# Attention scores of a gated cross-attention block: a second, turned score pass on TensorE replaced by row-wise exp on ScalarE, 32x32 turns on VectorE and block moves in SBUF

## The chip, the cores and the metric

The kernel runs on one NeuronCore of a Trainium2 chip. The metric is the device time of one execution in microseconds (us). The median of three runs of the kernel before is 1319.23 us (1318.6 to 1319.34).

## What is computed

The input x has 8 batches of 512 features by 2048 positions. Cut to what matters:

```python
# xattn: patches of W = 128 positions, H = 8 heads of dh = 32, DK = 256
q, k = Wq @ z + bq, Wk @ z + bk          # z = layernorm(x) over positions
val  = Wv @ ctx + bv
scores = einsum('bhdi,bhdj->bhij', qh, kh) / sqrt(dh)
scores = where(mask > 0, scores, -1e9)
attn = softmax(scores, axis=-1)
o = gelu(einsum('bhij,bhdj->bhdi', attn, vh))
x = x + tanh(g_x) * (Wo @ o + bo) * mask
# ffn: router over the positions of each row of layernorm(x), top 8 of 64 experts
logits = rows @ router.T + rb            # contraction over the 2048 positions
x = x + tanh(g_f) * (rows * w_sum + w_dense @ expert_bias)
```

The softmax of a patch and head is over j, along a row of the score matrix. The product with the values contracts over j, so it wants the weights with j on the partitions. The router contracts over positions, so it wants x with positions on the partitions.

## The kernel before

The work is cut into 64 units (`TU`), each of 256 positions (two patches, w = 0 and 1) of one batch. Eight units make a batch. There are five instruction streams, one for each engine and one for SyncE (SP) which issues the DMAs. Each stream is written in order by a loop over ticks: `SLOTS` gives every stage a place in a unit of 16 slots, unit u comes 16 slots after unit u - 1, and a negative or large number means an earlier or later unit's turn. The places set only the order in which an engine takes its work; the times come from semaphores. `ENDS` moves stages of the last units. Seven PSUM banks go round as a ring (`take`), given out ahead by the same places; `PR` is the eighth.

The stages of one unit, with their lines:

- `z_full` (L1115, GpSimd), `z_high` (L624, ScalarE) and `z_low` (L1122, GpSimd) make the normalised input and its two float32r parts. `project` (L316 to L318, TensorE) forms q and then k, 24 matmuls each; `q_full` (L632, ScalarE) and `k_full` (L806, VectorE) add the biases. The context goes through `c_high` (L640), `c_low` (L1128), `v_mm` (L331 to L333) and `v_full` (L646) the same way, twice per unit.
- `scores` (L347, L355, TensorE): mask rows `sel` times `ones3`, then q by k, 16 score tiles of 128x128 in four banks, query i on the partitions. `top` (L814, VectorE) takes the row maxima, `split` (L823 to L829) cuts them into three bf16 parts, `turn_max` (L367, TensorE) turns them, `max_turned` (L652, ScalarE) evicts them.
- `scores_turned` (L385, L392, TensorE) forms the scores again with key j on the partitions, mask and negated maxima added by matmuls. `expo` (L659, ScalarE) is four exps of 128x512 into `P`. `sums` (L403, TensorE) forms the denominators, `weigh` (L417) the product with the values. `invert` (L835, VectorE) is a reciprocal of 128x512, `divide` (L840) multiplies.
- `gelu` (L664) and `o_high` (L673) on ScalarE, `o_low` (L1139, GpSimd), `project_out` (L436 to L438, TensorE, two halves), `weigh_out` (L851, VectorE) and `add_x` (L1134, GpSimd) update x in place. Exp and gelu each load a table (`ACT_TABLE_LOAD`) in every unit.
- `r_full` (L684, ScalarE) centres the updated x, `r_turn` (L451, TensorE) turns it, `r_high` (L693, ScalarE) and `r_low` (L883, VectorE) split it, `r_mm` (L463, L464) adds it to the router's sum. `stats2` (L864) and `input_stats` (L967) are VectorE's statistics.
- Once per batch: the router's end (`c_logits` to `c_scale`, L699 to L940), `scale_x` (L720, ScalarE, four times 128x2048), `mix` (L500, L501, TensorE, 16 banks) and `add_mix` (L957, VectorE, 16), then 16 stores (L574) and, for the batch after next, 16 loads of x (L569), 256 KB each, issued by SP.

SP also issues per unit four small loads of mask rows into `sel` (L562), one of the mask (L553) and two of the context (L547).

Of the kernel before, what the change touches and what calls it, by code (L numbers as in the profile page):

```python
# [7 lines left out]
BF16 = mybir.dt.bfloat16  # L8
# [6 lines left out]
DT = D // 128  # L15
# [12 lines left out]
def bf16_parts(v):  # L28
# [23 lines left out]
    h=35.75, hT=39.75, hT_gap=0.25, ht_hi=42.25, ht_lo=44.5, R=49.75,  # L52

    norm2=25.25, c_base=28.75, L=33.25, LT=36.75, c_top=35.5, c_exp=37.25, c_w=41.25, c_sc=42.75, wT=40.5, wt_hi=41.25, wt_lo=42.5, mix=44.5, m_gap=0.25,
    sx=44.75, sx_gap=1.5, x2=46.5, rl=54.75, rl_gap=1,

    x_1=10.0, x_gap=3.75, bn1=66.75, bn1_gap=1.75, norm1=96.75,
# [13 lines left out]
G_IDENT, G_MXB = 2, 8  # L71


V_SUM, V_PICK, V_ROWS, V_SEL, V_ONES3, V_IDB, V_BQ = 3, 5, 9, 11, 12, 13, 14
V_KEEP, V_SW = 4, 7

TA = 1


def gated_block_kernel(nc, x, ctx, mask, g_x, g_f, wqT, wkT, wvT, woT, bq, bk, bv, bo, wrT, rb, eb, out):  # L80
    with ExitStack() as st:
# [9 lines left out]
        def f32(ap):  # L91
# [4 lines left out]
        NC, NV, NRW, NR, NO = 2, 4, 3, 7, 3  # L96
# [19 lines left out]
        P = sb("P", [128, 4, 2, 2, W])  # L116
        v32 = [sb(f"v32_{i}", [128, E]) for i in range(NV)]
        mx = [sb(f"mx{i}", [128, 4, 4]) for i in range(2)]
        mr = sb("mr", [128, 4, 4])
        mxb = sb("mxb", [128, 4, 8, 4], BF16)  # L120
        mxT = [sb(f"mxT{i}", [128, W], BF16) for i in range(2)]
        sel = [sb(f"sel{i}", [128, 4, W], BF16) for i in range(NRW)]
        pick = sb("pick", [128, 5])
        ones32 = sb("ones32", [128, DH])
# [3 lines left out]
        hc = [sb(f"hc{i}", [128, DT, U]) for i in range(2)]  # L128
# [9 lines left out]
        idb = sb("idb", [128, 128], BF16)  # L138
# [61 lines left out]
        s_pe, mx_v, part_v, mt_pe, mt_a, st_pe, exp_a, den_pe, pv_pe, rc_v, on_v = (sem(n) for n in (  # L200
            "S", "mx", "part", "MT", "mxT", "ST", "exp", "DEN", "PV", "rc", "on"))
        gelu_a, othi_a, otlo_g, wo_pe, xt_v, x1_g = (sem(n) for n in ("gelu", "othi", "otlo", "WO", "xt", "x1"))
        bn2_v, agg2_v, neg2_v, rstd2_g, h_a, ht_pe, hthi_a, htlo_v, r_pe = (sem(n) for n in (
            "bn2", "agg2", "neg2", "rstd2", "h", "hT", "hthi", "htlo", "R"))
# [6 lines left out]
        TICKS = range(-32 * 8, 8 * (128 * (NB + 1) + 96))  # L211
        SPLIT = -48
# [42 lines left out]
        for t in TICKS:  # L255
            for u in due(t, C["S"]):
                for g in range(4):
                    take(("S", 4 * u + g), t, C["top"] - C["S"] + g / 8, mx_v, 4 * u + g + 1)
# [34 lines left out]
        def _(e):  # L293
# [64 lines left out]
            def turn_max(u):  # L358
                _, freed, n = bank_of["MT", u]
                if freed:  # L360
                    e.wait_ge(freed, n)
# [851 lines left out]
```

## Time and profile before

| | |
|---|---|
| median of three runs | 1319.23 us |
| profiled execution, first to last instruction (span) | 1316.7 us |
| PE (TensorE) busy | 1273.2 us, 97% |
| DVE (VectorE) busy | 1004.8 us, 76% |
| ACT (ScalarE) busy | 893.3 us, 68% |
| POOL (GpSimd) busy | 712.7 us, 54% |
| DMA traffic | 116.15 MB, mean 88 GB/s |

The profiled execution is told by its span; no other time of it is given. The median of the runs is 2.5 us above that span. Busy times are of one engine each and overlap. A matmul's duration includes its way through the array, so the price of a group of matmuls is read from the start of one group to the start of the next.

### The profile page before, as it was taken

What the parts mean: (1) busy time and instruction counts of PE and PEld (TensorE: products, weight loads), DVE (VectorE), ACT (ScalarE), POOL (GpSimd) and SP (SyncE); (2) the same over time, 40 slices, a digit from 0 to 9 for tenths busy, and PEclk for the clock granted to TensorE, in tenths of its full rate; (3) what the DMA queues carried; (4) which work ended last, traced back from release to release, by engine and by line L of the source; (5) the groups of instructions that cost most, each with busy time, mean ns of one, the idle gap of its engine ahead of it and who ended that gap; (6) DMA issues with size and microseconds to landing.
All of it is one profiled execution on the core that took longest, in us unless ns stands there. A gap on an engine that the chain in (4) does not pass through costs nothing.

```text
span 1316.7 us, 37880 instructions
## 1 busy us (share of the span) xinstructions
PE 1273.2 (97%) x15313; PEld 1120.4 (85%) x15313; DVE 1004.8 (76%) x1871; ACT 893.3 (68%) x1600; POOL 712.7 (54%) x662
## 2 busy tenths in 40 slices
PE   3999999999999999999999999999999999999997
PEld 3898888889878889798887899878888798888875
DVE  6669768896788966888678776888768797687677
ACT  4676667677686676766667776676676766686755
POOL 2655664556645665456663655636664556654531
PEclk9999999999999999999999999999999999999999
DMA  9331111811136111451115411153111721123103
GB/s 277 110 104 43 34 42 51 262 40 39 43 102 216 36 39 35 149 170 43 34 43 165 154 32 42 34 192 128 43 35 38 242 78 43 34 78 114 34 6 128
DMA packets 120620, 116.15 MB, mean 88 GB/s; under 512 B 11392, under 2 KB 88320, under 8 KB 120320
## 3 DMA queue, kind: packets, MB, share of 16 engines
q1 hardware_dynamic: 119584, 113.74, 27.7%
q8 instruction: 122, 2.00, 0.6%
q14 instruction: 50, 0.41, 0.1%
q10 hardware_dynamic: 864, 0.01, 0.0%
HBM read 80.06 MB, written 33.65 MB: 86 GB/s over the span
## 4 chain that ended last, share of the span: by engine, by line
PE 84%; DVE 7%; ACT 5%; issue 2%; DMA 1%; POOL 0%; SPq 0%; DVEq 0%; ACTq 0%; POOLq 0%
PE ring L316 9%; PE ring L317 8%; PE ring L318 8%; PE ring L436 5%; PE ring L392 4%; PE ring L403 4%; PE ring L438 4%; PE ring L437 4%; PE ring L355 4%; PE ring L331 4%; PE ring L332 4%; PE ring L333 4%; PE ring L417 4%; PE ring L451 4%; PE PR L463 3%; ACT X L720 2%
## 5 line engine op out<-in xcount | busy, mean ns | idle before, releaser
L316 PE MATMUL ring<-z_hi,wqk_hi 128*128 128x256 f32 x1024 | 297.1, 290 | 21.8 <-DVE z_lo L1029 21.8
L1128 POOL TENSOR_TENSOR cx_lo<-cx,cx_hi 128x512 fp32r<-128x512 f32 x128 | 165.9, 1296 | 262.7 <-ACT cx_hi L640 262.7
L317 PE MATMUL ring<-z_hi,wqk_lo 128*128 128x256 f32 x1024 | 290.5, 284 | 0.0
L318 PE MATMUL ring<-z_lo,wqk_hi 128*128 128x256 f32 x1024 | 290.3, 283 | 0.0
L316 PEld LDWEIGHTS ring<-z_hi,wqk_hi 128*128 128x128 f32 x1024 | 197.1, 193 | 32.8 <-DVE wqk_lo L1004 21.8
L851 DVE SCALAR_TENSOR_TENSOR xt<-ring,cst,mg 128x256 f32<-128x256 f32 x256 | 112.0, 478 | 144.2 <-PE ring L438 144.2
L1122 POOL TENSOR_TENSOR z_lo<-z,z_hi 128x1024 fp32r<-128x1024 f32 x62 | 148.5, 2394 | 134.7 <-ACT z_hi L624 134.7
L835 DVE RECIPROCAL o<-ring 128x512 f32<-128x512 f32 x64 | 214.1, 3345 | 0.4 <-PE ring L403 0.4
L317 PEld LDWEIGHTS ring<-z_hi,wqk_lo 128*128 128x128 f32 x1024 | 197.3, 193 | 0.0
L318 PEld LDWEIGHTS ring<-z_lo,wqk_hi 128*128 128x128 f32 x1024 | 197.2, 193 | 0.0
L1134 POOL TENSOR_TENSOR X<-X,xt 128x512 f32<-128x512 f32 x128 | 163.7, 1282 | 42.6 <-DVE xt L851 32.1
L684 ACT ACTIVATE hc<-X,ln 128x256 f32<-128x256 f32 x256 | 109.2, 497 | 97.3 <-POOL X L1134 97.3
L814 DVE TENSOR_REDUCE mx<-ring 128x4 f32<-128x512 f32 x256 | 158.8, 682 | 20.7 <-PE ring L355 20.7
L632 ACT ACTIVATE q<-ring,cst 128x256 f32<-128x256 f32 x64 | 30.4, 476 | 208.0 <-PE ring L318 208.0
L331 PE MATMUL ring<-wv_hi,cx_hi 128*128 128x256 f32 x512 | 149.6, 292 | 1.0 <-POOL cx_lo L1128 1.0
L436 PE MATMUL ring<-ot_hi,wo_hi 128*128 128x256 f32 x504 | 148.5, 295 | 0.4 <-POOL ot_lo L1139 0.4
L332 PE MATMUL ring<-wv_lo,cx_hi 128*128 128x256 f32 x512 | 144.5, 282 | 0.0
L333 PE MATMUL ring<-wv_hi,cx_lo 128*128 128x256 f32 x512 | 144.2, 282 | 0.0
L438 PE MATMUL ring<-ot_lo,wo_hi 128*128 128x256 f32 x504 | 142.3, 282 | 0.0
L437 PE MATMUL ring<-ot_hi,wo_lo 128*128 128x256 f32 x504 | 141.3, 280 | 0.0
L1115 POOL TENSOR_SCALAR z<-X,ln 128x256 f32<-128x256 f32 x252 | 137.5, 558 | 0.0
L1139 POOL TENSOR_TENSOR ot_lo<-o,ot_hi 128x512 fp32r<-128x512 f32 x63 | 81.9, 1299 | 100.8 <-ACT ot_hi L673 100.8
(154 smaller groups left out, 3032.1 us busy)
## 6 DMA issues: line engine op xcount, KB each, us to landing
cx<-in_ctx SPq DMA_DIRECT2D x128, 256.0 KB, 2.7
out_y<-X SPq DMA_DIRECT2D x128, 256.0 KB, 3.0
X<-in_x SPq DMA_DIRECT2D x112, 256.0 KB, 5.2
mg<-in_mask SPq DMA_DIRECT2D x64, 128.0 KB, 3.0
X<-in_x SPq DMA_DIRECT2D x8, 512.0 KB, 7.5
sel<-rows_d SPq DMA_DIRECT2D x256, 3.0 KB
X<-in_eb SPq DMA_DIRECT2D x2, 512.0 KB, 7.9
X<-in_wqT SPq DMA_DIRECT2D x1, 512.0 KB, 6.1
```

The lines of the kernel that those rows point to most:

```text
L316: e.matmul(o, wqk_hi[:, t, cols], z_hi[:, t, :], t == 0, False)
L317: e.matmul(o, wqk_lo[:, t, cols], z_hi[:, t, :], False, False)
L318: last = e.matmul(o, wqk_hi[:, t, cols], z_lo[:, t, :], False, t == DT - 1)
L331: e.matmul(o, cx_hi[:, k, :], wv_hi[:, k, :], k == 0, False)
L332: e.matmul(o, cx_hi[:, k, :], wv_lo[:, k, :], False, False)
L333: last = e.matmul(o, cx_lo[:, k, :], wv_hi[:, k, :], False, k == DT - 1)
L436: e.matmul(o, wo_hi[:, m, cols], o_hi[:, m, :], m == 0, False)
L437: e.matmul(o, wo_lo[:, m, cols], o_hi[:, m, :], False, False)
L438: last = e.matmul(o, wo_hi[:, m, cols], o_lo[:, m, :], False, m == 1)
L835: e.reciprocal(o32[u % NO][:], bank("DEN", u)[:].rearrange("p (m i) -> p m i", m=2)).then_inc(rc_v, 1)
L1128: e.tensor_tensor(cx_lo[:], cx[p % NC][:], f32(cx_hi[:]), ALU.subtract).then_inc(cxlo_g, 1)
L1134: e.tensor_tensor(xs, xs, xt[j][:], ALU.add).then_inc(x1_g, 1)
```

## The change

Scores are formed once, with the query on the partitions. `top` writes negated maxima `nmx`. `expo` becomes 16 exps of 128x128 per unit, straight from the score banks, with the maximum as bias and the row sum as a second output (`accum_out`). VectorE turns the 32x32 blocks of `P` into `T` (`turn_p`, four times 128x512), inverts the 128x16 sums and turns them, spread over 512 columns (`turn_d`), and turns the updated x of unit u - 2 (`turn_h`, 128x1024). `move` on SP then puts the blocks in their places: 16 DMAs from `T` to `PT`, each of 32 partitions by 896 contiguous float32. `weigh` and `divide` read `PT`; `r_high` and `r_low` read the turned x there, and `r_low` goes to GpSimd. The centring of x (`r_full`) is dropped; the matching correction in `c_base` changes. For the last two units (`TF0` = 62 on) x is still turned by TensorE. The router's end of a batch comes 14.75 slots later (`late`), except in the last batch. All places in `SLOTS` and `ENDS` are new.

```diff
-    S=0.5, top=2.75, split=5.75, MT=7.75, mt_ev=9.75, ST=12.75, exp=16.25, DEN=18.25, PV=20.75, rc=19, on=21,
-    gelu=24, mg=5, ot_hi=25.25, ot_lo=29.25, WO=30, WO_gap=1.5, xt=32, x1=35.25, bn2=39.5,
+    rows=-11.5, z32=-25.5, z_hi=-20, z_lo=-14.75, q=-14.5, q_ev=-5.25, k=-11, k_ev=-7.5,
+    c_hi=-16.75, c_lo=-12.25, v=-12.25, v_ev=-5.5, v_gap=-2.75,
+    S=-1.25, top=4, exp=3.5, e_gap=0.25, tp=7, td=7.75, mv=7.25, PV=20, on=23.5,
+    gelu=22.25, mg=17, ot_hi=23.5, ot_lo=25, WO=29.5, WO_gap=3.25, xt=32.75, x1=34.5, bn2=44,
+    turn=39.25, t_hi=52, t_lo=55, t_R=55.75, t_gap=0.5, late=14.75,
...
-                    e.activation(P[:, g, :, :, :].rearrange("p m w i -> p (m w i)"), bank("ST", 4 * u + g)[:], ACT.Exp).then_inc(exp_a, 1)
+            def expo(u, g):
                 if u:
-                    e.wait_ge(pv_pe, u)
+                    e.wait_ge(tp_v, 4 * (u - 1) + g + 1)
+                e.wait_ge(nmx_v, 4 * u + g + 1)
+                for k in range(4):
+                    n = 4 * g + k
+                    last = e.activation(P[:, n, :], bank("S", 4 * u + g)[:, k * W:(k + 1) * W], ACT.Exp,
+                                        bias=nmx[u % 2][:, n:n + 1], accum_out=den[u % 2][:, n:n + 1])
+                last.then_inc(exp_a, 1)
...
+            def turn_p(u, g):
                 if u:
-                    e.wait_ge(mt_pe, u)
+                    e.wait_ge(pt_in, 256 * u)
+                e.wait_ge(exp_a, 4 * u + g + 1)
+                e.transpose(T[:, :, 4 * g:4 * g + 4, :].rearrange("p b k i -> p k b i"),
+                            P[:, 4 * g:4 * g + 4, :].rearrange("p k (b j) -> p k b j", b=4)).then_inc(tp_v, 1)
+
+            def turn_d(u):
+                e.wait_ge(exp_a, 4 * (u + 1))
+                e.reciprocal(rden[:], den[u % 2][:]).then_inc(rden_v, 1)
+                e.wait_ge(rden_v, u + 1)
+                if u:
+                    e.wait_ge(pt_in, 256 * u)
+                e.transpose(T[:, :, 16:20, :], rden[:].rearrange("p (b k) -> p b k", b=4).unsqueeze(3).to_broadcast([128, 4, 4, 32])).then_inc(td_v, 1)
...
+            def turn_h(u):
+                e.wait_ge(pt_in, 256 * (u + HLAG))
+                b, c = divmod(u, NU)
+                e.wait_ge(x1_g, 2 * (u + 1))
+                e.transpose(T[:, :, 20:28, :].rearrange("p q (w t) i -> p w q t i", w=2),
+                            X[b % 2][:, :, c * U:(c + 1) * U].rearrange("p t (w q i) -> p w q t i", w=2, q=4)).then_inc(turn_v, 1)
...
+            def move(u):
+                e.wait_ge(tp_v, 4 * (u + 1))
+                e.wait_ge(td_v, u + 1)
+                if u:
+                    e.wait_ge(on_v, u)
+                if u > HLAG:
+                    e.wait_ge(htlo_g, 2 * (u - HLAG))
+                n = 28 if u >= HLAG else 20
+                if u >= HLAG:
+                    e.wait_ge(turn_v, u - HLAG + 1)
+                for b in range(4):
+                    for a in range(4):
+                        e.dma_start(PT[32 * b:32 * b + 32, a, 0:n, :], T[32 * a:32 * a + 32, b, 0:n, :]).then_inc(pt_in, 16)
...
                 e.wait_ge(v_a, 2 * u + 2)
+                e.wait_ge(pt_in, 256 * (u + 1))
...
-                            last = e.matmul(o, v32[p % NV][:, h * DH:(h + 1) * DH], P[:, g, m, w, :], True, True)
+                            last = e.matmul(o, v32[p % NV][:, h * DH:(h + 1) * DH], PT[:, :, 4 * g + 2 * m + w, :], True, True)
```

## Rows read from the trace of the kernel before

**Rows 1.** Busy time by stretch: stretch, its length, then each engine busy (instructions), clock, DMA

```profile
649.53:667.86 18.33, 18.33 (x235) 16.50 (x234) 10.78 (x18) 12.48 (x23) 10.94 (x11) 1.00 0.14 38
...
530.45:689.22 158.77, 157.50 (x1910) 138.63 (x1910) 123.75 (x231) 110.13 (x198) 89.43 (x83) 1.00 0.28 88
```

**Rows 2.** Timeline of TensorE in a unit: start, length, engine, line, operation, count

```profile
658.70 0.23 PE L367 MATMUL ring<-idb,mxb 128*128 128x128 bf16 x1
...
659.57 0.36 PE L331 MATMUL ring<-wv_hi,cx_hi 128*128 128x256 f32 x1
...
661.16 0.40 PE L385 MATMUL ring<-mxT,sel 32*128 32x128 bf16 x16
...
662.44 0.38 PE L436 MATMUL ring<-ot_hi,wo_hi 128*128 128x256 f32 x1
...
665.51 0.39 PE L347 MATMUL ring<-sel,ones 32*128 32x512 bf16 x4
...
666.72 0.50 PE L463 MATMUL PR<-ht_hi,wr 128*128 128x512 f32 x1
...
667.86 1.06 PE L403 MATMUL ring<-P,ones 128*32 128x512 f32 x8
...
668.74 1.06 PE L417 MATMUL ring<-P,v 128*32 128x128 f32 x32
```

**Rows 3.** Groups by line: count, busy us, mean ns of one, idle before

```profile
L659 ACT ACTIVATE P<-ring 128x512 f32<-128x512 f32 x256 | 132.2, 604 | 2.2 <-PE ring L392 1.5
...
L684 ACT ACTIVATE hc<-X,ln 128x256 f32<-128x256 f32 x256 | 109.2, 497 | 97.3 <-POOL X L1134 97.3
...
L720 ACT ACTIVATE X<-X,sc 128x2048 f32<-128x2048 f32 x31 | 64.1, 2096 | 1.4 <-DVE sc L940 1.3
```

**Rows 4.** Timeline of ScalarE: small exps with row sums, once per batch

```profile
217.46 0.35 ACT L704 ACTIVATE ex<-lg,sc 128x64 f32<-128x64 f32 x1
...
217.79 0.34 ACT L704 ACTIVATE ex<-lg,sc 128x64 f32<-128x64 f32 x1
```

**Rows 5.** Timeline of ScalarE in a mid-batch unit

```profile
656.02 0.63 ACT L640 ACTIVATE cx_hi<-cx 128x512 fp32r<-128x512 f32 x1 [0.54 <-PE ring L333]
...
656.67 1.28 ACT L664 ACT_TABLE_LOAD   x1
...
658.78 0.36 ACT L646 ACTIVATE v<-ring 128x256 f32<-128x256 f32 x1
...
659.04 0.62 ACT L673 ACTIVATE ot_hi<-o 128x512 fp32r<-128x512 f32 x1
...
659.56 0.26 ACT L652 ACTIVATE mxT<-ring 128x128 bf16<-128x128 bf16 x1
...
659.72 1.08 ACT L693 ACTIVATE ht_hi<-ring 128x512 fp32r<-128x512 f32 x2
```

**Rows 6.** DMA issues by line: KB each, median us to landing

```profile
out_y<-X SPq DMA_DIRECT2D x128, 256.0 KB, 3.0
```

**Rows 7.** Timeline of the DMA queue issued by SyncE

```profile
385.79 12.50 SPq L574 DMA_DIRECT2D out_y<-X  x16
...
414.96 1.40 SPq L562 DMA_DIRECT2D sel<-rows_d  x4
```

**Rows 8.** Busy time in a stretch where stores and loads of x overlap

```profile
416.00:420.00 4.00, 4.00 (x65) 2.62 (x58) 3.62 (x7) 1.80 (x5) 3.87 (x6) 1.00 1.03 382
```

**Rows 9.** Timeline of GpSimd and VectorE: an operation with two SBUF inputs

```profile
377.46 1.30 POOL L1128 TENSOR_TENSOR cx_lo<-cx,cx_hi 128x512 fp32r<-128x512 f32 x1 [3.98 <-ACT cx_hi L640]
...
377.61 1.44 DVE L925 TENSOR_TENSOR ex<-ex,lr 128x256 f32<-128x256 f32 x1
```

**Rows 10.** Timeline of VectorE in the last unit

```profile
1265.37 2.48 DVE L814 TENSOR_REDUCE mx<-ring 128x4 f32<-128x512 f32 x4 [0.38 <-PE ring L355]
...
1274.42 3.36 DVE L835 RECIPROCAL o<-ring 128x512 f32<-128x512 f32 x1 [0.41 <-PE ring L403]
...
1277.88 0.69 DVE L840 TENSOR_TENSOR o<-ring,o 128x512 f32<-128x512 f32 x1
```

More of the change, by code:

```diff
@@ L229, in batch, with after @@
             return due(t, 128 + lag, 128, NB)
+        def after(t, lag):
+            return due(t, 128 + lag + C["late"], 128, NB - 1) + tuple(b for b in due(t, 128 + lag, 128, NB) if b == NB - 1)
         def o_parts(u):
@@ L257, in gated_block_kernel @@
                 for g in range(4):
-                    take(("S", 4 * u + g), t, C["top"] - C["S"] + g / 8, mx_v, 4 * u + g + 1)
+                    take(("S", 4 * u + g), t, end("exp", u) + C["e_gap"] * (g + 1) - C["S"], exp_a, 4 * u + g + 1)
             for u in due(t, C["q"]):
@@ L265, in gated_block_kernel @@
                     take(("v", 2 * u + w), t, C["v_ev"] - C["v"], v_a, 2 * u + w + 1)
-            for u in due(t, C["MT"]):
-                take(("MT", u), t, end("mt_ev", u) - C["MT"], mt_a, u + 1)
-            for u in due(t, C["ST"]):
-                for g in range(4):
-                    take(("ST", 4 * u + g), t, end("exp", u) - C["ST"] + g / 2, exp_a, 4 * u + g + 1)
-            for u in units(t, "DEN"):
-                take(("DEN", u), t, end("rc", u) - end("DEN", u), rc_v, u + 1)
             for u in units(t, "PV"):
@@ L410, in weigh @@
                 e.wait_ge(v_a, 2 * u + 2)
+                if u == TU - 1:
+                    keep_on(bank("PV", u)[:], 2)
+                e.wait_ge(pt_in, 256 * (u + 1))
                 for w in range(2):
@@ L599, in _ @@
                     load_weight(u)
+                for u in units(t, "mv"):
+                    move(u)
                 for w in range(2):
@@ L776, in _ @@
                         v_full(2 * u + w)
-                for u in units(t, "mt_ev"):
-                    max_turned(u)
-                for u in units(t, "exp"):
-                    expo(u)
+                for g in range(4):
+                    for u in units(t, "exp", C["e_gap"] * g):
+                        expo(u, g)
                 for u in units(t, "gelu"):
@@ L1083, in _ @@
                     for u in units(t, "ht_lo", C["hT_gap"] * a):
-                        r_low(u, a)
+                        if u >= TF0:
+                            r_low(u, a)
+                for u in due(t, C["turn"], count=TF0):
+                    turn_h(u)
                 for b in batch(t, C["c_base"]):
                     c_base(b)
-                for b in batch(t, C["c_top"]):
+                for b in after(t, C["c_top"]):
                     c_top(b)
-                for b in batch(t, C["c_w"]):
+                for b in after(t, C["c_w"]):
                     c_weights(b)
-                for b in batch(t, C["wt_lo"]):
+                for b in after(t, C["wt_lo"]):
                     if b == NB - 1:
@@ L1094, in _ @@
                     w_low(b)
-                for b in batch(t, C["c_sc"]):
+                for b in after(t, C["c_sc"]):
                     if b < NB - 1:
@@ L1098, in _ @@
                 for i in range(16):
-                    for b in batch(t, C["x2"] + C["m_gap"] * i):
+                    for b in after(t, C["x2"] + C["m_gap"] * i):
                         add_mix(b, i // 4, i % 4)
@@ L1181, in _ @@
                         add_x(u, j)
+                for a in range(2):
+                    for u in due(t, C["t_lo"] + C["t_gap"] * a, count=TF0):
+                        r_low(u, a)
                 for b in batch(t, C["norm2"]):
```

277 lines of the change are left out of this document (103 added, 174 removed), and 10 rows, old and new, of the table ENDS.

## Prediction

> **What bounds the kernel now.** I read the busy time by stretch first. One mid-batch unit lasts 18.33 us and TensorE is busy for all of it; a whole batch lasts 158.77 us with TensorE busy for 157.50, ScalarE 110.13, VectorE 123.75, GpSimd 89.43, at a granted clock of 1.00 (2.4 GHz) [rows 1]. So TensorE's own work sets the end, and a batch costs 158.77 - 8 x 18.33 = 12.1 us more than eight mid-batch units: the router's end, the mix and the stores. The timeline of TensorE then gives the price of each group from its start to the start of the next [rows 2]. Waits of the other engines cost nothing today, so most of what matters after the change, the waits between engines, can't be read off as idle time; it has to be put together from durations and the new order.
>
> **What TensorE loses.** Turning the maxima and turning x takes from 658.70 to 659.57, 0.87 us; the second score pass from 661.16 to 662.44, 1.28; the sums from 667.86 to 668.74, 0.88 [rows 2]. Together 3.03 us of 18.33, so TensorE's floor is 15.3 us a unit and 158.8 - 24.2 = 134.5 a batch. (Two units of 64 keep the turn of x: under 2 us in all.) The product with the values keeps its count; its moving operand is now four pieces of 32 columns in a row, between nothing and the 1.06 us that the group lasts once more [rows 2]; I take nothing, since a contiguous piece of 128 bytes is long beside one column.
>
> **What ScalarE gains.** Out go four exps of 0.604 and four centrings of 0.497 [rows 3] and one eviction of 0.26 [rows 5]: 4.7 us. In come 16 exps of 128 columns with bias and row sum. The trace has this form with 64 columns: it starts every 0.33 us, 217.46 to 217.79, its accumulator read included [rows 4]. For the 64 columns more I add the slope between the 256-column and the 2048-column ACTIVATE with a pointer bias, (2.096 - 0.497) / 1792 = 0.9 ns a column [rows 3], so 0.39 us each and 6.2 us in all; bounds are 5.3 (no slope) and 8.0 (0.497 each, as for 256 columns). ScalarE's occupancy of 12.48 [rows 1] becomes at least 14.0; consecutive ACTIVATEs overlap by some 0.1 us, so the eight that go were worth less than their durations, and I take 14.7.
>
> **VectorE and GpSimd.** The reciprocal of 3.36 us goes, with the four small splits and two subtractions of 128x512. Five turns of 128x512 and one of 128x1024 come. No row shows a turn; the nearest is the 128x512 multiply of 0.69 us [rows 10]. A turn can't write faster than such an operation reads, and twice as slow is the other end, so the turns cost 4.6 to 9.2 us. I take 4.6, as the data is one stream in and one out. So VectorE stays near 124 us a batch, under the floor of TensorE. GpSimd takes over two subtractions at 1.30 us [rows 9]: 10.94 [rows 1] becomes 13.5.
>
> **SyncE and the moves.** Each unit issues 16 DMAs of 32 x 3584 bytes, 1.84 MB. Four small ones take 1.40 us to issue, 0.35 each, and 16 stores of 256 KB take 12.50 us, 0.78 each [rows 7], and a store lands after 3.0 us [rows 6]. So a move lasts between 16 x 0.35 + 3.0 = 8.6 and 12.5 + 3.0 = 15.5 us; the stores are held by VectorE's adds, and the bytes alone at the 382 GB/s seen [rows 8] are 4.8 us, so I take 10. Behind the move on SP's queue stand the context loads, the mask rows, and once a batch the stores and loads of x.
>
> **The unit's length after the change.** With every engine under 15.3 us of work, order decides. I followed the new places modulo 16 slots. TensorE goes S(u), second half of WO(u-2), q, v, PV(u-1), k, R, v, first half of WO(u-1), S(u+1). ScalarE goes exp 0 to 2, first r_high, exp 3, c_high, second r_high, gelu(u-1), o_high(u-1), evictions, z_high. WO(u-1) stands ahead of S(u+1), and gelu(u-1) behind the exps of u. That closes a loop: S 1.21 us, 665.51 to 666.72 [rows 2]; first row maximum 2.48 / 4 = 0.62 [rows 10]; table load 1.28 [rows 5]; exps 6.2; two r_high, c_high, table load, gelu and o_high, which in the trace stand from 656.02 to 660.80, less 0.26 for v (658.78 to 659.04) and 0.16 for mxT (659.56 to 659.72), 4.36 [rows 5]; o_low on GpSimd 1.30 [rows 9]; half of the output projection, (665.51 - 662.44) / 2 = 1.5 [rows 2]. The sum is 16.5, and for the tail of a matmul group behind its last start, 1.06 - 0.88 = 0.18 [rows 2] twice, I add 0.4: 16.9 us. A second path, r_low and c_low on GpSimd and then v on TensorE, reaches WO(u-1) at the same moment. So 18.33 falls to 16.9, and less than half of TensorE's saving arrives.
>
> **The batch's end.** Today it adds 12.1 us. ScalarE adds 4 x 2.10 [rows 3] and some 2.5 for small exps and two evictions, and has 16.9 - 14.7 = 2.2 to spare, so at least 8.7 us; the 16 adds of VectorE, at 0.6 each, come out like that too. The stores and loads of x, 8.4 MB, now share the queue with 1.84 MB per unit, and the DMA engines already show a busy share of 1.03 there [rows 8]. I take 13, bounds 9 and 18.
>
> **Start and end.** In the last unit the chain from the first maximum to the division lasts from 1265.37 to 1278.57, 13.2 us, with a reciprocal of 3.36 in it [rows 10]. The new one is 0.62 + 6.2 + turns 1.6 + move 10 + product 1.06 + division 0.69, some 20. Less one centring on the path, the end gets 6 us longer.
>
> **Sum.** A batch is 8 x 16.9 + 13 = 148.2, 10.6 less than 158.8. Eight batches: -85; the end: +6. The span goes from 1316.7 to 1238, and with the 2.5 us by which the median lies above the profiled span, 1240 us.
>
> **Rivals.**
>
> *A, the loop through ScalarE* as summed. With 16.4 to 17.5 a unit and 9 to 18 a batch it gives 1178 to 1318, most likely 1190 to 1300. For it speaks that it needs only durations that the trace has; against it, that I timed no other loop as closely. 0.50.
>
> *B, the waits are hidden.* If the exps cost nearer 5.3 us and the order lets o_low come in time, TensorE bounds again: 1316.7 - 8 x 24.2 + 6 + 2.5 = 1131 at the lowest, to 1180. For it speaks that four engines have less than 15.3 us each; against it, that ScalarE's part of the loop alone is 13 of the 15.3. 0.20.
>
> *C, the moves bound, slower than before.* `T` is a single buffer: the next unit's turns wait for the landing of the whole move, and the move waits for all of them. The turns, the division between them and the small reciprocal are 5.3 us, so a unit is 5.3 plus the move. Up to a move of 11.6 us it is hidden behind A; from 12.8 us the unit is 18.1 and the kernel is no faster. At 14 us the unit is 19.3, a batch 167, and the time 1394. For it: the queue's other traffic, and that each DMA covers 32 partitions only, which no row shows at this size. Against: 1.84 MB is 4.8 us of bytes. 0.12. The Trainium skill, SBUF — State Buffer, section on Door 1 (the DMA port swizzle), has partitions 0 to 31 reach 8 of the 16 ports, 189 GB/s at 1 MiB; an estimate by that page is 9.7 + 3.0 = 12.7 us for a move, a unit of 18.0 and a time of about 1311. No run here shows it yet.
>
> *D, turns and GpSimd hold each other.* At 377.61 a VectorE operation that elsewhere is short lasts 1.44 us and ends just after GpSimd's of 377.46 to 378.76 [rows 9]. VectorE's sources were mostly PSUM; the turns read and write SBUF. If each of the six waits half of a GpSimd operation at 80% occupancy, 0.5 us, VectorE loses 3 us, and the loop, which passes GpSimd too, some 1.4: a unit of 18.3, a batch of 159.4, 1330 us. Against it: a turn has one source. 0.09. The Trainium skill, SBUF — State Buffer, section "SBUF: two separate sides", calls that port pair an exclusive lock, taken by an operation in a two-port mode or with two SBUF inputs; rows 9 agree (1.44 us) for two inputs. It does not say which a turn is.
>
> *E, the batch's end grows.* If the queue of stores, loads and moves runs behind by 10 us or more, a batch's end costs 26: 161.2 a batch, 1348 us, with 18 to 26 in between. 0.09.
>
> **How the numbers follow.** The likeliest is A, 1240. Low end: B's middle parts are taken in, 1140. High end: D and half of E, 1330; C's upper part and the lowest of B, under 2 in 10 together, stay out. Within 0.2% is about what a measurement of this kernel can't tell from no change. Faster: A and B nearly whole, a third of E and small parts of C and D, 0.77. Same 0.03. Slower: the rest, 0.20.
>
> **What would show it.** Right if a mid-batch unit of the changed kernel lasts about 16.9 us, TensorE waits before the output projection for o_low, the 16 exps start 0.39 us apart, a turn of 128x512 lasts 0.6 to 0.7, and the moves land some 10 us after the first issue. The loop is wrong if TensorE has no wait longer than 0.3 us (B), if VectorE's turns wait for DMAs (C), if turns last over 1 us beside GpSimd (D), or if only the batch ends are long (E). A clock under 1.00 in the new gaps would make all of it longer; nothing idle for more than 2 us is in my sum mid-batch, and the clock held through today's short ones [rows 1].

## The result, and the profile after

The changed kernel takes 1323.6 us (median of 10 runs, 1317.5 to 1328.4), the kernel before 1318.8 us beside it. The ratio is 1.0032 with a 95% interval of 1.0018 to 1.0046: slower by 0.3%. The prediction was 1240 us and faster; the time lies in the range of 1140 to 1330, the direction was wrong.

The page of the changed kernel: busy time by engine, the granted clock in 40 slices, and the chain that ended last by engine and by line.

```profile
PE 1123.9 (85%) x11165; PEld 1010.7 (76%) x11165; DVE 968.2 (73%) x1859; ACT 1004.8 (76%) x3072; POOL 871.4 (66%) x784
...
PEclk9899999999999899999999999989999989999979
...
SPq 36%; DVE 18%; PE 12%; DMA 10%; ACT 10%; issue 9%; POOL 5%; DVEq 0%; ACTq 0%; POOLq 0%
SPq L551 33%; DMA PT<-T 8%; ACT P L643 7%; DVE T L797 5%; DVE T L806 2%; POOL ht_lo L1118 2%; DVE X L936 2%; DVE o L812 2%; DVE nmx L790 2%; DMA cx<-in_ctx 1%; ACT L643 1%; PE ring L475 1%; SPq L556 1%; PE ring L343 1%; DVE bnst L946 1%
```

TensorE lost 149 us of work (1273.2 before) and nothing came of it: no engine is busy for more than 85% of the span, and a third of the chain is line 551, where SyncE issues the DMAs of the move. TensorE's mean clock went from 0.999 to 0.963. The same page's groups of instructions and its DMA issues, for the prices that the prediction had put together:

```profile
L643 ACT ACTIVATE P<-ring,nmx 128x128 f32<-128x128 f32 x1024 | 360.6, 389 | 2.1 <-DVE nmx L790 1.3
...
L797 DVE STREAM_TRANSPOSE T<-P 128x512 f32<-128x512 f32 x256 | 170.8, 687 | 135.9 <-DMA PT<-T 134.9
...
PT<-T SPq DMA_DIRECT2D x992, 112.0 KB, 2.3
```

The waits of the changed kernel, longest first (engine and line, what it waited for, us in total, times, longest):

```profile
ACT L643 <- DVE nmx L790: 171.0, 61, 7.2
...
DVE T L797 <- DMA PT<-T: 134.9, 51, 8.4
...
PE ring L384 <- DMA PT<-T: 87.8, 52, 6.2
ACT ht_hi L667 <- DMA PT<-T: 50.2, 41, 12.1
```

Three engines wait for the same DMAs: VectorE to turn the next weights into `T`, TensorE for the product with the values, ScalarE to split the turned x. (The first row is no loss of the move: in four_moves, below, it is 163.8.)

Busy time by stretch, a mid-batch unit and a batch, to be read against [rows 1]:

```profile
635.05:652.56 17.51, 15.72 (x170) 14.19 (x170) 12.16 (x21) 14.22 (x46) 13.48 (x13) 1.00 0.59 140
652.56:808.57 156.01, 137.11 (x1389) 123.46 (x1390) 118.77 (x229) 124.08 (x382) 109.89 (x99) 0.98 0.70 184
```

TensorE's work is what was forecast: 15.7 a unit (15.3), 137.1 a batch (134.5); ScalarE's 14.2 (14.7); GpSimd's 13.5 (13.5). What is wrong is not the work but the order's length. The timeline of SyncE's queue, against [rows 7]:

```profile
648.51 10.55 SPq L551 DMA_DIRECT2D PT<-T  x16
659.11 0.59 SPq L520 DMA_DIRECT2D cx<-in_ctx  x1
...
660.81 1.33 SPq L535 DMA_DIRECT2D sel<-rows_d  x4
```

and VectorE's in the same unit:

```profile
643.35 1.30 DVE L797 STREAM_TRANSPOSE T<-P 128x512 f32<-128x512 f32 x2 [3.60 <-DMA PT<-T]
644.58 1.20 DVE L854 STREAM_TRANSPOSE T<-X 128x1024 f32<-128x1024 f32 x1
...
647.74 0.71 DVE L806 STREAM_TRANSPOSE T<-rden 128x512 f32<-128x512 f32 x1
...
660.72 1.30 DVE L797 STREAM_TRANSPOSE T<-P 128x512 f32<-128x512 f32 x2 [3.46 <-DMA PT<-T]
```

The turns start at 643.35, the last is done at 648.5, SyncE issues from 648.51 to 659.06, 0.66 us each, and at 660.72 the next turns start: 5.16 us of turns and 12.2 us of move, 17.4 us. That is rival C's formula, "5.3 plus the move", with a move of 12.2 instead of 10. This move is one of the shorter ones: over the 40 middle units (16 to 55) the median from the first issue to the last landing is 12.6 us, and the mid-batch units are 17.7 us long on average.

At the end of a batch it is worse. SyncE's queue there, then TensorE's timeline, then the busy time of two stretches (the last three numbers are clock, share of the DMA engines, GB/s):

```profile
431.94 0.53 SPq L561 DMA_DIRECT2D out_y<-X  x1
432.51 0.47 SPq L556 DMA_DIRECT2D X<-in_x  x1
433.15 10.56 SPq L551 DMA_DIRECT2D PT<-T  x16
```

```profile
447.92 1.94 PE L384 MATMUL ring<-PT,v 128*32 128x128 f32 x32 [6.18 <-DMA PT<-T]
```

```profile
440.00:445.00 5.00, 1.74 (x15) 1.53 (x13) 4.97 (x10) 3.71 (x16) 1.14 (x1) 1.00 0.99 208
445.00:450.00 5.00, 2.08 (x33) 1.73 (x34) 2.19 (x3) 3.90 (x21) 3.55 (x6) 0.63 0.93 290
```

The turns were done at 430.9. Stores and loads of x stand ahead until 433.0, 16 issues last until 443.7, the DMA engines are busy for 0.93 to 0.99, and the move is there at 447.9: 17 us. TensorE waits 6.2 us, and the 32 products behind the wait take 1.94 us, where in a mid-batch unit they take 1.08. The granted clock of that stretch is 0.63 on average, most of it at the lower level of 1.2 GHz, after 1.00 in the stretch in which TensorE stopped.

Where the time is, by the starts of the score products on TensorE's timeline (`four_moves` is an experiment below in which the move takes four DMAs):

| us | before | after | four_moves |
|---|---|---|---|
| start to the first scores | 32.8 | 32.7 | 32.2 |
| first 8 units | 139.0 | 148.4 | 133.9 |
| next 48 units (six batches) | 951.8 | 944.3 | 880.0 |
| last 7 units | 140.4 | 134.8 | 127.7 |
| last scores to the end | 52.8 | 66.2 | 62.6 |
| span | 1316.7 | 1326.4 | 1236.3 |

Where before a batch was 8 x 18.3 + 12.1, after it is four units of 17.7 and four, around the batch's end, of 21.6 (86.5 together): 157.4. A batch gains 1.4 us on [rows 1], 7.5 in six of them; the first 8 units lose 9.4, the last 7 gain 5.6, and the end loses 13.4.

### The profile page after: what moved, and what is told of

Read it like the earlier page. It is cut to its first block, busy times and chain, and to the rows that moved or that the text cites. A ratio compares the mean times of both kernels' runs of the same rounds, so it can differ in the third digit from the quotient of the medians.

```text
span 1326.4 us, 32364 instructions
## 1 busy us (share of the span) xinstructions
PE 1123.9 (85%) x11165; PEld 1010.7 (76%) x11165; DVE 968.2 (73%) x1859; ACT 1004.8 (76%) x3072; POOL 871.4 (66%) x784
## 4 chain that ended last, share of the span: by engine, by line
SPq 36%; DVE 18%; PE 12%; DMA 10%; ACT 10%; issue 9%; POOL 5%; DVEq 0%; ACTq 0%; POOLq 0%
SPq L551 33%; DMA PT<-T 8%; ACT P L643 7%; DVE T L797 5%; DVE T L806 2%; POOL ht_lo L1118 2%; DVE X L936 2%; DVE o L812 2%; DVE nmx L790 2%; DMA cx<-in_ctx 1%; ACT L643 1%; PE ring L475 1%; SPq L556 1%; PE ring L343 1%; DVE bnst L946 1%
## 5 line engine op out<-in xcount | busy, mean ns | idle before, releaser
L643 ACT ACTIVATE P<-ring,nmx 128x128 f32<-128x128 f32 x1024 | 360.6, 389 | 2.1 <-DVE nmx L790 1.3
L328 PE MATMUL ring<-z_hi,wqk_hi 128*128 128x256 f32 x1024 | 302.1, 295 | 24.8 <-DVE z_lo L1000 21.1
L329 PE MATMUL ring<-z_hi,wqk_lo 128*128 128x256 f32 x1024 | 294.3, 287 | 0.0
L797 DVE STREAM_TRANSPOSE T<-P 128x512 f32<-128x512 f32 x256 | 170.8, 687 | 135.9 <-DMA PT<-T 134.9
L1118 POOL TENSOR_TENSOR ht_lo<-PT,ht_hi 128x512 fp32r<-128x512 f32 x124 | 160.1, 1292 | 133.7 <-ACT ht_hi L667 133.5
L643 ACT ACTIVATION_READ_ACCUMULATOR P<-ring,nmx 128x1 f32 x1024 | 234.5, 229 | 0.0
L328 PEld LDWEIGHTS ring<-z_hi,wqk_hi 128*128 128x128 f32 x1024 | 200.9, 196 | 38.9 <-DVE wqk_lo L975 21.1
L329 PEld LDWEIGHTS ring<-z_hi,wqk_lo 128*128 128x128 f32 x1024 | 201.2, 196 | 0.6
L790 DVE TENSOR_REDUCE nmx<-ring 128x4 f32<-128x512 f32 x256 | 158.7, 682 | 19.1 <-PE ring L367 19.1
L403 PE MATMUL ring<-ot_hi,wo_hi 128*128 128x256 f32 x504 | 153.6, 305 | 4.4 <-POOL ot_lo L1111 4.4
L384 PE MATMUL ring<-PT,v 128*32 128x128 f32 x2048 | 74.5, 289 | 89.7 <-DMA PT<-T 87.8
```

Source lines behind the costliest of these rows:

```text
L328: e.matmul(o, wqk_hi[:, t, cols], z_hi[:, t, :], t == 0, False)
L329: e.matmul(o, wqk_lo[:, t, cols], z_hi[:, t, :], False, False)
L403: e.matmul(o, wo_hi[:, m, cols], o_hi[:, m, :], m == 0, False)
L643: last = e.activation(P[:, n, :], bank("S", 4 * u + g)[:, k * W:(k + 1) * W], ACT.Exp, bias=nmx[u % 2][:, n:n + 1], accum_out=den[u % 2][: ...
L790: e.tensor_reduce(nmx[u % 2][:, 4 * g:4 * g + 4], bank("S", 4 * u + g)[:].rearrange("p (k j) -> p k j", k=4), AX.X, ALU.max, negate=True). ...
L797: e.transpose(T[:, :, 4 * g:4 * g + 4, :].rearrange("p b k i -> p k b i"), P[:, 4 * g:4 * g + 4, :].rearrange("p k (b j) -> p k b j", b=4) ...
```

## The experiments

**What a DMA of the move costs.** The first kernel computes nothing; it issues groups of transfers of several shapes, one group after the other.

```
for b in range(4):
    for a in range(4):
        e.dma_start(dst[32*b:32*b+32, a, 0:n], T[32*a:32*a+32, b, 0:n])   # n = 896, 640, 448, 1024, 64
```

> This kernel leaves out the whole computation and only issues transfers from SyncE: groups of 16 with 32 partitions by 896, 640, 448, 1024 and 64 float32 from SBUF to SBUF, 8 with 64 partitions by 896, 4 with 128 partitions by 896, 16 with 128 by 224, and 16 stores of 128x512, each group twice and each waiting for the one before. In the changed kernel a transfer of 32x896 takes 0.66 us of SyncE's queue (10.55 us for 16), where the prediction had 0.35. Theory I (a fixed price of issuing a transfer from SBUF to SBUF): 0.6 to 0.7 us for every width, 64 columns too, and for 64 or 128 partitions, so four of 128x896 are issued in 2.6 us. Theory W (the width: the queue is held back by the bytes in flight, 114.7 KB in 0.66 us is 174 GB/s): the 32-partition groups follow their width, 0.33 for 448 and under 0.3 for 64, and four of 128x896 still need 10 us. Theory Q (the price comes from the busy kernel around it): 0.35 us for all of them here.

SyncE's queue in that kernel; line 36 is 896 columns, 56 is 64 columns, 61 is eight DMAs of 64 partitions x 896, 65 four of 128 x 896:

```profile
7.29 10.15 SPq L36 DMA_DIRECT2D dst<-T  x16
...
53.66 10.28 SPq L56 DMA_DIRECT2D dst<-T  x16
65.15 7.04 SPq L61 DMA_DIRECT2D dst<-T  x8
75.78 2.95 SPq L65 DMA_DIRECT2D dst<-T  x4
```

Sixteen issues take 10.0 to 10.3 us, 0.63 each, with 114 KB in each or with 8. So for 32 partitions the price belongs to the DMA and not to its bytes. It isn't the same for every shape: with 64 partitions the first three issues take 0.5 to 0.6 us and the later ones 0.85 to 1.10, 0.88 on average, and four of 128 x 896 take 0.74 each. The next group starts only when the last has landed, so the starts give the whole move: 11.8 us (7.29 to 19.08) for 16 DMAs, 10.6 (65.15 to 75.78) for 8, and 6.2 for 4 (the group after starts at 81.97).

**Half the bytes, or fewer DMAs.** Three kernels change the move alone; their outputs aren't the reference's, since blocks are left out or not exchanged between partitions.

```
half_bytes:   n = 14 if u >= HLAG else 10                  # was 28 and 20; the rest of PT is zeroed once
eight_moves:  e.dma_start(PT[64*b:64*b+64, a, 0:n, :], T[64*b:64*b+64, a, 0:n, :])   # b < 2, a < 4
four_moves:   e.dma_start(PT[:, a, 0:n, :], T[:, a, 0:n, :])                         # a < 4
```

> The changed kernel with each of the 16 moves of a unit cut to half its width (14 of 28 columns of blocks); the rest of the turned weights, the sums and the turned x isn't moved, so that part of the computation is left out. The order, the waits and the number of transfers stay. Theory I (issuing 16 transfers bounds): a mid-batch unit stays at 17.4 to 17.9 us and the time within 1% of 1323. Theory W (bytes or ports bound): the move falls from 12.2 to about 7.5 us, the unit to the loop through ScalarE, 16.9, and the time to about 1250.

> The changed kernel with the same bytes moved by 8 transfers of 64 partitions that leave the blocks in their own partitions, so the placing of the blocks is left out and the numbers that come out are others. Theory I: 8 x 0.66 + 2.3 = 7.6 us for a move instead of 12.2, so it is hidden, and the unit falls to the loop through ScalarE, 16.9 us; time about 1250. Theory W: bytes and partitions per port are as before, the unit stays at 17.4 to 17.9 and the time within 1% of 1323.

> The same with 4 transfers of 128 partitions. Theory I: a move of 2.6 + 2.3, at least the 4.8 us that the bytes take, so about 7 us; well hidden, the time as with eight, about 1240 to 1250, since the loop through ScalarE (16.9 us a unit) takes over. If that loop doesn't exist, the time falls toward TensorE's floor, 1131. Theory W with all 128 partitions at work: also about 7 us, so this run tells apart the next bound, not I from W.

| kernel | us | ratio to before, 95% interval | batch | last scores to end | move |
|---|---|---|---|---|---|
| after | 1323.6 | 1.0018 to 1.0046 | 157.4 | 66.2 | 12.6 |
| half_bytes | 1304.0 | 0.9869 to 0.9909 | 154.7 | 63.6 | 12.2 |
| eight_moves | 1266.6 | 0.9586 to 0.9626 | 151.1 | 61.8 | 11.9 |
| four_moves | 1237.5 | 0.9368 to 0.9399 | 146.7 | 62.6 | 6.6 |

(The last column is the median over units 16 to 55 from the first issue of a move to its last landing.)

SyncE's queue in half_bytes, eight_moves and four_moves:

```profile
653.47 10.71 SPq L551 DMA_DIRECT2D PT<-T  x16
```

```profile
650.33 7.48 SPq L551 DMA_DIRECT2D PT<-T  x8
```

```profile
488.87 2.93 SPq L550 DMA_DIRECT2D PT<-T  x4
```

Half the bytes take as long to issue and give 20 us of 86; the same bytes in four DMAs give all of it. Two expectations were missed here. half_bytes came out 1.5% under the changed kernel, where theory I had said within 1%: the bytes have a small part. eight_moves was to have a move of 7.6 us and a time of about 1250; its issues take 7.0 us, but the last one lands 4.7 us later, so the move is only 0.75 us shorter than with sixteen. That it still gives 57 us fits a loop that each unit passes: 5.2 us of turns and 11.9 of move are 17.1, close to the 16.8 at which the move is hidden, and 0.75 us in each of 64 units is 48 us. Fewer DMAs are also wider ones, so these two kernels change two things at once; twoq below leaves all sixteen as they are and changes only who issues them.

With four, VectorE waits for no move any more, TensorE once for 1.1 us and ScalarE once for 7.1, a unit lasts 16.8 us (predicted 16.9) and a batch 146.7 (148.2), and the kernel takes 1237.5 where 1240 was predicted: with the move out of the way the rest of the sum comes out right, in part because its errors cancel (see below). Its chain of waits, by engine, and one unit of it:

```profile
ACT 35%; PE 30%; POOL 13%; DVE 13%; issue 7%; DMA 1%; SPq 0%; DVEq 0%; POOLq 0%; ACTq 0%
```

```profile
476.94 0.95 PE ring L367 x32
...
477.98 0.70 DVE nmx L789
478.75 1.28 ACT L642
...
480.99 1.29 ACT P L642 x8
...
484.34 0.52 ACT ht_hi L666
...
486.25 0.52 ACT cx_hi L628
...
487.44 1.28 POOL ht_lo L1117
488.72 1.25 POOL cx_lo L1099
```

The scores, one row maximum, the table load, the exps with one split of x among them, then c_high, the second split, r_low and c_low on GpSimd, v and half of WO on TensorE until the next scores at 493.44: 16.8 us. This is the prediction's "second path"; the first, through gelu and o_low, isn't in the chain, but it ends only 0.2 us earlier: o_low is done at 491.61, and TensorE starts the output projection at 491.77. The prediction had said that both reach it at the same moment.

```profile
490.31 1.30 POOL L1110 TENSOR_TENSOR ot_lo<-o,ot_hi 128x512 fp32r<-128x512 f32 x1 [0.35 <-ACT ot_hi L658]
```

**Is it that loop?** four_moves with four exps of 512 columns without row sums in place of 16 (the weights are then not those of the reference, and the sums are set to one).

```
last = e.activation(P[:, 4*g:4*g+4, :].rearrange("p k j -> p (k j)"), bank("S", 4*u+g)[:], ACT.Exp,
                    bias=nmx[u % 2][:, 4*g:4*g+1])
```

> The kernel with four moves, and in it four exps of 128x512 instead of 16 of 128x128: the row sums aren't taken and the maximum of one head serves four, so that part of the computation is left out. With four moves a mid-batch unit is 16.8 us and the waits show the transfers no longer. Theory A (the loop scores, maximum, exps, gelu, output projection, scores bounds there): 16 exps cost 5.4 us, four cost 2.0, so the loop is 13.4 us and the unit falls to TensorE's floor of about 15.3, a batch from 146.7 to about 136, the time from 1237 to about 1150. Rival (something else holds 16.8, as ScalarE's total work or the batch's end): the unit falls by under 0.5 us and the time by under 30 us.

1179.3 us (0.8922 to 0.8961). Mid-batch units are 15.2 us, the floor of TensorE that the prediction had at 15.3. So once the move is hidden, ScalarE's exps set the unit, and 16 of them cost 58 us of the kernel against four. The expected 1150 was not reached: a batch takes 140.2 us and not 136, and what holds its end was not tried.

**Through which door does the move hold the unit?** `T` is single (VectorE), but PT is late for TensorE and ScalarE too, and the context loads stand behind the move. xpe leaves x to TensorE in all units and the low part of its split to VectorE, so a DMA moves 32 x 640; xpe_two_t has two buffers `T` on top; after_cx and xpe_two_t_cx have ScalarE issue the context loads.

```
xpe:        TF0 = 0;  n = 20                                # was TU - HLAG; 28
xpe_two_t:  T = [sb(f"T{i}", [128, 4, 20, 32]) for i in range(2)]
            if u > 1: e.wait_ge(pt_in, 256 * (u - 1))       # turns; was: if u: e.wait_ge(pt_in, 256 * u)
*_cx:       load_ctx(e, 2*u+2) behind c_high(2*u+1), load_ctx(e, 2*u+3) four slots ahead of the unit, both on ScalarE
```

> The changed kernel, complete, with one part undone: x is turned by TensorE in every unit, not only the last two, so the turn of x (1.2 us) leaves the loop of turns and moves, the moves are 32x640, and the split goes back to VectorE. Theory I: the issue price doesn't depend on the width, so the move stays 12.2 to 13 us and the unit falls by the turn alone, 1.2 us, to about 16.5; time about 1245 to 1265. Theory W (bytes): the move falls by 8/28 too, to about 9.5, and the unit to the next bound, about 16.1 (TensorE has 0.8 us more work); time about 1215.

> The whole result is computed. x is turned by TensorE as in xpe, each DMA moves 32 x 640, all 16 go through SyncE, and there are two buffers T (640 columns each, one output buffer o32 fewer to make room). So the turns of a unit wait for the landing of the move before the last, no longer for the last one. Theory C, the move counts because T is single (unit = turns + move): the waits of the turns for PT vanish, although SyncE still needs 10 us for 16 issues and some 3.5 us for its loads; units of 15.9 to 16.9 us, as with two queues, and 1265 to 1280 us. Rival, SyncE's issue time holds by itself (the move, the loads and the stores in one queue, about 14 us a unit and more at a batch's end): the gain is under 5 us and the kernel stays at 1293 to 1300 us.

> The whole result is computed. As xpe_two_t (1299 us), with the context loads issued by ScalarE. There no turn waits for a move any more and the time did not fall; in the chain of its trace the 16 issues are followed by the landing of a context load, its split, gelu and o_high. If the loads behind the move are what holds it, the units get to 15.9 to 16.3 us and the kernel to 1270 to 1280 us, what xpe_twoq has. If the placed weights themselves arrive too late for the product with the values, it stays at 1293 to 1300 us.

> The whole result is computed. The changed kernel, with the 126 context loads of the loop issued by ScalarE (behind the split of the second half, and four slots ahead of the next unit) instead of by SyncE behind the move; all 16 DMAs of the move stay on SyncE. Theory C alone (unit = turns + move through the single T): the loads are not on that loop, SyncE's issues stay 10.6 us, so mid-batch units stay near 17.7 us and the kernel within 5 us of 1323. Rival, SyncE's queue as a whole (what stands behind the move arrives late and holds ScalarE's splits, 35.5 us of waits in the changed kernel's trace): 1300 to 1312 us, most of it at the batch ends.

| kernel | us | 95% interval of the ratio |
|---|---|---|
| xpe | 1298.3 | 0.9834 to 0.9876 |
| xpe_two_t | 1299.3 | 0.9846 to 0.9879 |
| xpe_two_t_cx | 1286.3 | 0.9726 to 0.9772 |
| after_cx | 1321.1 | 0.9987 to 1.0033 |

The expectation for xpe was missed by 33 us and more: its moves, 29% lighter, take 10.8 us to issue (784.49 to 795.26) as before. Two buffers took most of VectorE's wait away, from the first of these rows (xpe) to the second (xpe_two_t), and the time stayed, so the loop through the single `T` is not all that makes the move count:

```profile
DVE T L793 <- DMA PT<-T: 81.2, 34, 5.5
```

```profile
DVE T L793 <- DMA PT<-T: 20.2, 35, 1.0
```

The chain of xpe_two_t shows the next door: behind the last issue comes a context load, its split, and gelu on ScalarE, and only then o_low.

```profile
658.59 4.16 DMA cx<-in_ctx
662.83 0.63 ACT cx_hi L625
663.48 1.28 ACT L646
...
665.77 0.64 ACT ot_hi L655
666.48 1.29 POOL ot_lo L1108
```

With the loads on ScalarE that door is open and 13 us come, half of what four issues less on SyncE bring (xpe_two_t_q, below); the expectation had 1270 to 1280 if this door were the last, or no gain, and the time lies between. In the changed kernel itself the same edit gives nothing beyond the noise (after_cx), as expected: its turns still wait for `T`, and VectorE waits 147.3 us for the move there, 134.9 without the edit.

So there are at least two doors one behind the other, and opening the first alone gives nothing. xpe_two_t_cx still lies 12 us over xpe_two_t_q, which has the shorter move. The traces point to a third door, the late arrival of PT itself: TensorE waits for it 21.1 us in 23 places in xpe_two_t_cx and 0.7 us in one in xpe_two_t_q. That it is worth these 12 us was not tried by itself.

**A second queue.** ScalarE issues a part of the 16 DMAs (four; eight in the last unit).

```
SyncE:    place(e, u, range(0, 2 if u == TU - 1 else 3))
ScalarE:  place(e, u, range(2 if u == TU - 1 else 3, 4))    # at slot 12.5; twoq8_tail: 2 and 2 in all units
twoq_tail:  ("mva", 1): 4.25                                # was -5: behind gelu and o_high of unit 62
```

> The changed kernel, complete: SyncE issues 12 of the 16 moves of a unit, ScalarE the other 4, at a place where it waits for the next maxima (in the last unit 8 and 8). Theory I (SyncE's price of 0.63 to 0.69 us per issue is what makes the move long): the move falls from 12.2 to 13 us to 12 x 0.66 + 2.3 = 10.2, the loop of turns and moves from 17.4 or more to 15.4, and the unit to 16.8 or, as ScalarE now has 2.4 us more of work, 17.1; time 1250 to 1270. If the two queues share one issuing unit, so that ScalarE's four and SyncE's twelve cost one after the other what sixteen did, the time stays within 1% of 1323.

> Both together, complete. The loop of turns and moves is then 10.2 + 4.0 = 14.2 us and far from binding; two r_high have left the stretch between the exps and gelu, so the loop through ScalarE is 15.7; TensorE's floor is 16.1. Unit 16.1 to 16.4, a batch 142, time about 1205 to 1225, faster than the kernel before by 7 to 9%. If it comes out above 1240, ScalarE's total (its old work, the exps and four issues) bounds instead.

> The whole result is computed. As xpe_two_t, with 4 of the 16 DMAs issued by ScalarE. If SyncE's queue holds the batch ends (stores, loads of x and moves in one queue), this gains over both xpe_two_t and xpe_twoq (1273): 1250 to 1265 us. If the batch ends of these kernels are held by their order of work on TensorE, ScalarE and VectorE, with a move that is hidden, it comes out within 5 us of 1273.

> The whole result is computed. As twoq, but ScalarE's 8 issues of the last unit stand behind gelu and o_high of unit 62 instead of ahead of them. In twoq the last scores start at 1202.4 and the end comes 71.3 us later, against 62.5 us in four_moves; TensorE waits 13.6 us there for o_low of unit 62, which stands behind ScalarE's issues. If these issues are what makes the tail long, it falls by 7 to 9 us: 1268 to 1271 us. If the tail waits for the landing of the last move in any case, it stays within 2 us of 1277.

> The whole result is computed. As twoq_tail (1269 us), with the context loads issued by ScalarE. Its mid-batch units are 16.8 us already; its batch is 150.3 us against 146.6 in four_moves, where SyncE has four issues a unit. If late context loads at the batch ends are that difference, a batch falls to 147 to 148.5 and the kernel to 1248 to 1258 us. If it is the move itself behind stores and loads of x, it stays within 4 us of 1269.

> The whole result is computed. As twoq_tail (1269 us), with 8 of the 16 DMAs of every unit on SyncE and 8 on ScalarE; the context loads are on SyncE again. If the rest of the batch ends (150.3 us a batch against 146.6 in four_moves) is SyncE's 12 issues in the way of stores and loads, a batch gets near 148 and the kernel to 1248 to 1258 us. If ScalarE's issues cost its own work anything (four of them overlapped its ACTIVATEs and cost no time mid-batch), the units leave 16.8 us and it gets slower than 1269: at 0.3 us for each of the four more, 1.2 us a unit, 1340.

| kernel | us | 95% interval | mid-batch unit | batch | last scores to end |
|---|---|---|---|---|---|
| twoq | 1277.3 | 0.9666 to 0.9703 | 16.8 | 151.2 | 71.3 |
| xpe_twoq | 1273.2 | 0.9632 to 0.9663 | 15.9 to 16.3 | 149.9 | 71.2 |
| xpe_two_t_q | 1274.2 | 0.9645 to 0.9674 | 15.9 to 16.3 | 151.1 | 69.9 |
| twoq_tail | 1269.5 | 0.9608 to 0.9644 | 16.8 | 150.4 | 63.0 |
| twoq_tail_cx | 1264.3 | 0.9573 to 0.9613 | 16.8 | 149.7 | 62.8 |
| twoq8_tail | 1327.4 | 1.0041 to 1.0072 | 17.9 | 158.8 | 64.6 |

Four issues less on SyncE bring the unit to loop A's 16.8 at once, with the same sixteen DMAs of the same shape and the whole result computed. This is the cleanest evidence that issuing is what makes the move too long: the bytes and partitions are those of the changed kernel, and the move's median falls from 12.6 to 10.4 us. With that shorter move a second `T` gives nothing either (xpe_two_t_q beside xpe_twoq), so it is not `T` that holds their batch ends. But twoq came out 7 us over what was expected of it, and its end is why: ScalarE's eight issues of the last unit stood ahead of gelu of unit 62, and TensorE waited for what follows it. ScalarE, then TensorE, in twoq:

```profile
1214.25 6.70 ACTq L526 DMA_DIRECT2D PT<-T  x8
1220.98 1.28 ACT L653 ACT_TABLE_LOAD   x1 [8.32 <-issue]
```

```profile
1225.30 0.58 PE L403 MATMUL ring<-ot_hi,wo_hi 128*128 128x256 f32 x1 [13.55 <-POOL ot_lo L1116]
```

Behind gelu they cost 8 us less, as expected (twoq_tail). Context loads off SyncE's queue bring the batch 0.7 us and the kernel 5, under the 11 to 21 expected, with intervals that overlap a little. Eight issues on each queue, which looked like the even split, are slower than the kernel before. It isn't that the two queues issue one after the other: in the unit shown SyncE's eight stand beside ScalarE's, which last from 645.01 to 650.90; each issue takes 0.74 to 0.77 us instead of 0.66, and all sixteen are out in 7.1 us:

```profile
643.78 6.17 SPq L526 DMA_DIRECT2D PT<-T  x8
```

ScalarE in twoq, then in twoq8_tail:

```profile
634.68 0.52 ACTq L526 DMA_DIRECT2D PT<-T  x1
...
635.93 1.26 ACTq L526 DMA_DIRECT2D PT<-T  x2
637.29 0.63 ACT L632 ACTIVATE cx_hi<-cx 128x512 fp32r<-128x512 f32 x1 [0.50 <-issue]
```

```profile
646.23 4.67 ACTq L526 DMA_DIRECT2D PT<-T  x6
651.00 0.63 ACT L632 ACTIVATE cx_hi<-cx 128x512 fp32r<-128x512 f32 x1 [3.88 <-issue]
```

The first issues run beside ACTIVATEs that are already under way (v, q and z_high, 634.75 to 636.8); from then on the engine stands still until the last is out. Four cost 0.5 us here and 29.9 in 47 such waits over the kernel; eight cost 3.9 here and 206.2 in 54 waits. xpe_twoq has three units of 15.9 to 16.3 us in each batch and wins little for it: the units beside them take 19 to 20.5, and a batch 149.9 against 150.4 in twoq_tail. That missed its expectation by 48 us and more. Which order of work holds these units stays open.

## Why the prediction was wrong

- **The step that failed is the size of the move.** "Four small ones take 1.40 us to issue, 0.35 each ... I take 10." An issue of the move costs 0.63 alone and 0.66 in the kernel, 16 of them 10.6, and 1.7 us pass from the last issue to the next turn: 12.2 us in the unit shown, 12.6 in the median, and 17 at a batch's end counted from the last turn. That is within the stated 8.6 to 15.5 mid-batch, but past the 11.6 up to which it was hidden. The bytes, by which I had pulled the value down, have no part in the issue time: 64 columns cost what 896 do. The lower bound was taken from four transfers of 3 KB. The trace of the kernel before has nine loads in a row at its start, 0.4 to 0.7 us apart, and they were a nearer row, though 16 of those and the 3.0 of a landing are 11.4 us, which would still have been hidden.
- **Rival C was the case, at 0.12.** Its formula gives 5.2 + 12.2 = 17.4 a unit, 17.8 with the median move, and the traces have 17.5 to 17.7. It decided against itself by its break-even, 18.1 us a unit, and that is right mid-batch: after's middle units are shorter than before's 18.3. With a unit of 17.4 in place of 16.9 and nothing else changed the forecast's sum gives 1272 us, still faster than before. What it left out is that the same queue is longer where stores and loads of x share it, and that the move counts in the first batch and at the end too.
- **The batch's end**, "I take 13, bounds 9 and 18", measured 157.4 - 8 x 17.7 = 15.8, and with the move out of the way (four_moves) 146.7 - 8 x 16.8 = 12.3. The stores, the loads and the moves do meet (17 us for one move at 430.9), which was rival E in kind, but at 3 us and not at 10. (E's time, 1348, was a slip: by its own terms 161.2 a batch gives 1344.)
- **The end of the kernel**, +6 predicted, +13.4 measured. From the first row maximum to the end of the division: 1261.64 to 1288.67, 27.0 us for the predicted 20 and the 13.2 of [rows 10]. 4.2 us are a wait of the turns for the move of unit 62, which the sum lacked, and the last move takes 12.5 from its first issue until its landing. four_moves has +9.8 too, though its move is short, so some 4 us of the miss are not the move. In its chain the 16 exps with two splits of x among them (6.7 us), then gelu, o_high and o_low of unit 62 stand in a row before the output projection; which of them is worth what was not tried.
- **The first batch**: taken as one of eight alike; it lost 9.4 us where the others gained 1.4. TensorE's granted clock from 30 to 180 us is 0.93, and 1.00 before. Its own cause was not tried, but it goes with the move: four_moves has 133.9 us there, eight_moves 133.7, and twoq and twoq_tail, with sixteen DMAs on two queues, 134.4 and 138.2. "The clock held through today's short ones" did not carry: waits of 2 to 6 us came in, and the granted clock was 0.63 in the 5 us in which the longest shown here ended. What the clock is worth alone can't be told from these runs.
- **Right in mechanism, and in size partly by luck: loop A**, 16.9 predicted and 16.8 with the move hidden. The exps were mis-sized: 0.39 from start to start was predicted, 0.34 is measured (0.39 is how long one ACTIVATE lasts), so 16 of them cost 5.4 us and not 6.2, near the stated lower bound of 5.3. The other steps of the loop came out 0.7 longer together (in four_moves 4.8 for the splits, gelu and o_high instead of 4.36, 1.8 for half of the output projection instead of 1.5, 0.1 to 0.2 at each change of engine), and the two cancel. The sign "TensorE waits before the output projection for o_low" did not show: 4.4 us in all in the changed kernel.
- **Right**: TensorE's and GpSimd's work, and the turn (0.69 predicted, 0.687 measured; 128 x 1024 1.20).
- **Rival D is out**: the 256 turns of 128 x 512 last 661 to 714 ns, and the 171 of them that overlap a GpSimd operation 687 on average, like the 85 that don't (686); a turn that waited for half a GpSimd operation would be near 1.2 us. The Trainium skill, SBUF — State Buffer, section "SBUF: two separate sides", has the port pair taken by operations with two SBUF inputs or in a two-port mode; by these rows a turn of fp32 takes no such lock.
- The Trainium skill's estimate for the move (SBUF — State Buffer, Door 1), 12.7 us, came nearer than mine, but not for its reason: by port bandwidth the 9.7 us of transfer would have been fourteen times shorter with 64 columns than with 896, and the sixteen issues took 10.28 us against 10.15.

The account, by the table of starts and against the forecast span of 1238: the six middle batches are 6 x (157.4 - 148.2) = 55 us over (38 in the length of the units, 17 in the batch's end), the first batch 20 and the last seven units 5 (each was to be 10.6 shorter than before), the end 7. Together that is the profiled span of 1326.4. Only the move was changed in four_moves, and it takes 1237.5.

## What to carry to other kernels

Count the DMAs before their bytes: a step that becomes sixteen transfers occupies the queue that issues them for sixteen issues, here 0.6 us each for 32 partitions whatever the width, and everything behind them in that queue is late by the sum. Price a burst from the longest burst of the trace, and where a price lies near the point from which a rival decides, give that rival the weight. Before a second queue gets its part, look at what the engine that owns it does next: four issues fitted beside ScalarE's work and made the kernel 3% faster (twoq; 4% with its last unit and the context loads placed better, 1264 us), eight made it slower than before.

## What the runs showed of the hardware

- An issue back to back on one queue: 0.63 us for 32 partitions x 64 to 1024 columns from SBUF to SBUF (16 in 10.0 to 10.3 us), 0.88 for 64 partitions x 896 and 0.74 for 128 x 896; the four 3 KB loads of mask rows 0.33 to 0.35 ([rows 7] and the changed kernel).
- Two queues issue beside each other: eight DMAs on SyncE and eight on ScalarE are out in 7.1 us, each at 0.74 to 0.77 us, where sixteen on one queue take 10.6.
- Turns of 32x32 blocks on VectorE, fp32, SBUF to SBUF: 0.69 us for 128 x 512 and 1.20 for 128 x 1024, with or without GpSimd at work beside them.
- DMAs issued by ScalarE run beside ACTIVATEs already under way, and the next ACTIVATE waits until the last is out (0.5 us for four, 3.9 us for eight).
- A table load of 1.28 us stands twice in each unit (exp, gelu) and is on the loop: in four_moves at 478.75.
